# Turning quantised weights with DMA transposes from SBUF to SBUF in a recurrent network with a feed-forward block

## The reference

```python
xW = einsum('ntd,dh->nth', x, Wx) + b               # x: (2, 2048, 512)
h_t = tanh(xW_t + h_{t-1} @ Wh)                     # 2048 steps, h_0 = cond_1024
def quant_linear(x, w, b):                          # w: one scale for each row
    s_in = max(max(x), EPS) / 255;  xq = clip(round(x / s_in), 0, 255) * s_in
    s_w = max(max|w| over a row, EPS) / 127;  wq = clip(round(w / s_w), -128, 127) * s_w
    bq = round(b / (s_in * s_w)) * s_in * s_w
    return xq @ wq.T + bq
hidden = relu(quant_linear(h, w1, b1))              # w1: (2048, 512)
y = x + quant_linear(hidden, w2, b2)                # w2: (512, 2048)
```

## Time and profile before

| | before |
|---|---|
| median of 3 runs | 517.89 us (517.83 to 518.94) |
| the profiled execution | 517.75 us |
| its span | 515.9 us |
| mean granted TensorE clock | 0.996 of full |
| TensorE busy | 496.1 us, 96% of the span |
| VectorE, ScalarE, GpSimd busy | 310.6, 256.5, 55.8 us |
| share of TensorE in the chain that ended last | 93% |

### The profile page before, as it was taken

The page is one execution under the profiler, slowest core; times in us unless marked ns, Lnnn a source line. Parts: engine busy times, 40 slices in busy tenths (PEclk is TensorE's granted clock), DMA queues, the critical chain, the costliest instruction groups (busy, mean ns, idle before and its releaser), DMA issues.

```text
span 515.9 us, 9080 instructions
## 1 busy us (share of the span) xinstructions
PE 496.1 (96%) x2954; PEld 300.8 (58%) x2954; DVE 310.6 (60%) x587; ACT 256.5 (50%) x455; POOL 55.8 (11%) x41
## 2 busy tenths in 40 slices
PE   8999999999999999999857999999998999999997
PEld 3444555555599999999845444444444444444442
DVE  0988880000033344545677988888687687778776
ACT  0434444444233332323478555555554776676661
POOL 2000000000000000000000000000000543534455
PEclk9999999999999999999999999999998999999999
DMA  8988510000000000000000577300002088888883
GB/s 293 323 314 297 176 70 1 0 1 1 0 0 0 0 0 0 0 0 0 1 2 3 213 295 307 164 0 1 0 0 81 2 285 269 304 291 323 287 315 123
DMA packets 21142, 61.19 MB, mean 119 GB/s; under 512 B 2032, under 2 KB 2176, under 8 KB 17536
## 3 DMA queue, kind: packets, MB, share of 16 engines
q1 hardware_dynamic: 20448, 59.84, 31.9%
q10 hardware_dynamic: 576, 1.05, 0.6%
q0 software_dynamic: 96, 0.01, 0.0%
HBM read 39.93 MB, written 20.97 MB: 118 GB/s over the span
## 4 chain that ended last, share of the span: by engine, by line
PE 93%; DVE 3%; ACT 2%; issue 1%; DVEq 0%
PE bank L468 22%; PE bank L637 22%; PE bank L677 21%; PE bank L493 11%; PE bank L499 11%; PE bank L483 3%; PE bank L515 2%; PE bank L448 1%; DVE arena L1037 1%; PE bank L464 1%; ACT arena L824 1%; ACT w1t L737 0%; DVE arena L1238 0%; DVE arena L1262 0%; DVE acc_max L1198 0%
## 5 line engine op out<-in xcount | busy, mean ns | idle before, releaser
L468 PE MATMUL bank<-arena 128*128 128x512 f32 x256 | 116.2, 602 | 0.2 <-DMA arena<-wx 0.2
L637 PE MATMUL bank<-arena,w1t 128*128 128x512 bf16 (+1 forms) x512 | 110.9, 379 | 1.2 <-DVE arena L1167 1.2
L677 PE MATMUL bank<-arena,w2t 128*128 128x512 bf16 x512 | 111.4, 379 | 0.5 <-DVE arena L1262 0.5
L433 POOL TENSOR_SCALAR arena<-arena,bq 128x512 f32<-128x512 f32 x32 | 53.1, 1672 | 446.8 <-DVEq L1283 393.5
L637 PEld LDWEIGHTS bank<-arena,w1t 128*128 128x128 bf16 x512 | 49.9, 98 | 61.9 <-issue 1.4
L677 PEld LDWEIGHTS bank<-arena,w2t 128*128 128x128 bf16 x512 | 49.1, 98 | 62.6 <-DVE arena L1262 4.8
L1198 DVE TENSOR_REDUCE acc_max<-arena 128x2 f32<-128x1024 f32 x60 | 71.6, 1217 | 15.8 <-ACT arena L875 15.2
L468 PEld LDWEIGHTS bank<-arena 128*128 128x128 f32 x256 | 47.3, 192 | 51.4 <-issue 50.3
L875 ACT COPY arena<-bank 128x1024 f32<-128x1024 f32 x56 | 56.7, 1012 | 40.2 <-PE bank L637 40.2
L899 ACT ACTIVATE arena<-arena,bias,scale 128x512 uint16 (+1 forms) x93 | 69.9, 807 | 9.0 <-DVE arena L1250 8.3
L994 DVE TENSOR_TENSOR arena<-bank,arena 128x128 f32 x48 | 14.0, 292 | 91.5 <-PE bank L499 91.2
(11 more groups left out here) (96 smaller groups left out, 314.7 us busy)
## 6 DMA issues: line engine op xcount, KB each, us to landing
spill<-arena SPq DMA_DIRECT2D x12, 1024.0 KB, 3.9
arena<-spill SPq DMA_DIRECT2D x12, 1024.0 KB, 8.9
arena<-w SPq DMA_DIRECT2D x8, 1024.0 KB, 5.3
arena<-x_t SPq DMA_DIRECT2D x32, 256.0 KB, 3.8
y_t<-arena SPq DMA_DIRECT2D x32, 256.0 KB, 2.1
arena<-x_t SPq DMA_DIRECT2D x7, 1024.0 KB, 8.6
arena<-x_t ACTq DMA_DIRECT2D x4, 256.0 KB, 5.8
arena<-wx SPq DMA_DIRECT2D x4, 256.0 KB, 5.2
```

The source lines that it names most:

```text
L433: nc.gpsimd.tensor_scalar(xb[:, d], xb[:, d], bq2[:, d:d + 1], None, ALU.add).then_inc(xb_ready, 1)
L468: return nc.tensor.matmul(bank[:, j, :], wx_sb[:, k, j * P:(j + 1) * P], x_in[:, X_ORDER[i], k, :], start=(k == 0), stop=(k == KT - 1))
L637: mm = nc.tensor.matmul(bank[:, f % 8, :], w1t[:, k, f * P:(f + 1) * P], q[:, slot, k, :], start=(k == 0), stop=(k == KT - 1))
L677: return nc.tensor.matmul(bank[:, 4 + d, :], w2t[:, f, d * P:(d + 1) * P], hq[:, f % HQ_RING, :], start=(f == 0), stop=(f == FT - 1))
```

## The change

- The integers of w1 are written row by row to `w1_ints`, which is the space of `w2t`; those of w2 to `w2_ints`, in the area of the first two x groups that TensorE uses. So VectorE first waits until these 8 units of x products are done.
- SP issues 16 DMA transposes for w1, each 128x512 bf16 from `w1_ints` to `w1t`, four behind each of the x and w2 loads of groups 4 to 7. When all 16 have landed, it issues 4 for w2, each 128x2048 bf16, from `w2_ints` to `w2t`.
- TensorE waits for all of `w2t` before the recurrence, since the states go over `w2_ints`.
- `turn_weights`, `store_turned`, the bf16 identity and their semaphores are gone. In the first joint TensorE does 7, 2 and 5 idle products, in the second 6, 2 and 9, the first 6 ahead of the transpose of `s_hid` and after the last kept bank.

```diff
+IDLE_STATES = (7, 2, 5)
+IDLE_HIDDEN = (6, 2, 9)
+IDLE_BANK = 7
...
+        w1_ints = w2t
+        x_done = x_in[:, X_ORDER[0]:X_ORDER[0] + 2]
+        assert X_ORDER[1] == X_ORDER[0] + 1
+        w2_ints = x_done.bitcast(BF16).rearrange("p g k t -> p (g k t)").rearrange(
+            "p (i f) -> p i f", i=KT)
...
                 load_x(i, i % 2)
                 load_w(i, i % 2, (w_in[:, i % 2, :], w2_v[i - 4]))
 
+                sp.wait_ge(w_int_ready, i - 3)
+                for n in range(4 * (i - 4), 4 * (i - 3)):
+                    nc.sync.dma_start_transpose(w1t[:, :, n * P:(n + 1) * P],
+                                                w1_ints[:, n, :]).then_inc(w1_turned, 16)
+
+            sp.wait_ge(w1_turned, 16 * FT)
+            for i in range(KT):
+                sp.wait_ge(w_int_ready, 4 + i + 1)
+                nc.sync.dma_start_transpose(w2t[:, :, i * P:(i + 1) * P],
+                                            w2_ints[:, i, :]).then_inc(w2_turned, 16)
+
...
             nc.gpsimd.memset(ones[:, :], 1.0).then_inc(ones_set, 1)
-            pool.wait_ge(small_in, 32)
-            nc.gpsimd.tensor_copy(id16[:, :], id32[:, :]).then_inc(id16_set, 1)
...
-                if unit in TURN_BEHIND:
-                    if TURN_BEHIND[unit] == 0:
-                        pe.wait_ge(id16_set, 1)
-                        pe.wait_ge(ones_set, 1)
-                    pe.wait_ge(w_int_ready, TURN_BEHIND[unit] + 1)
-                    for a in range(4):
-                        n = 4 * TURN_BEHIND[unit] + a
-                        turn_weights(n, 4 + a, after=(n - 4 if n >= 4 else None))
...
+            pe.wait_ge(w2_turned, 16 * KT)
             pe.wait_ge(xw_free, KT + GROUPS * KT)
             main_pass(0)
...
-            turn_middle(0, 11)
-            spread_stat(0, lambda: turn_middle(11, 13))
-            turn_middle(13, MIDDLE - EARLY)
+            def keep_going(n):
+                idle_products(n, IDLE_BANK, w1t[:, 0, 0:P], w1t[:, 0, 0:GTOK])
+
+
+            pe.wait_ge(fixed_ready, 2 * FIXED)
+            keep_going(IDLE_STATES[0])
+            spread_stat(0, lambda: keep_going(IDLE_STATES[1]))
+            keep_going(IDLE_STATES[2])
             pe.wait_ge(flag_ready, 1)
...
             all_kept = ACC_RING + GROUPS * PAIRS - len(HELD) // 2
-            pe.wait_ge(acc_kept, all_kept - 1)
-            turn_late(0, 1)
+            pe.wait_ge(acc_kept, all_kept)
+            keep_going(IDLE_HIDDEN[0])
             pe.wait_ge(hid_ready, 1)
             nc.tensor.transpose(bank[0:1, 4, 0:P], s_hid[:, :], id32[:, :]).then_inc(hid_turned, 1)
-            pe.wait_ge(acc_kept, all_kept)
-            turn_late(1, ring)
+            keep_going(IDLE_HIDDEN[1])
             pe.wait_ge(hid_row, 1)
             nc.tensor.matmul(bank[:, 4, P:P + 1], ones[:, :], stat_row[:, 0:1], start=True,
                              stop=True).then_inc(hid_spread, 1)
-            turn_late(ring, TURNED - MIDDLE)
-
-            pe.wait_ge(w_stored, MIDDLE + 2)
-            idle_products(IDLE_BARRIER, LATE_BANKS[1], w1t[:, 0, 0:P], w1t[:, 0, 0:GTOK])
-            pe.wait_ge(w_stored, TURNED)
+            keep_going(IDLE_HIDDEN[2])
             pe.wait_ge(scales1_ready, 1)
...
-            for i in range(MIDDLE - EARLY):
-                store_turned(EARLY + i, MIDDLE_BANKS[i % len(MIDDLE_BANKS)])
             act.wait_ge(flag_ready, 1)
...
-                linked(nc.vector.tensor_scalar(turned, ints, ROUND, None, ALU.subtract), w_link,
+                linked(nc.vector.tensor_scalar(ints, flat, ROUND, None, ALU.subtract), w_link,
                        g * W_LINKS + 6)
...
+            dve.wait_ge(xw_acc, 2 * KT)
             with dve.Fori(2, 4) as half:
                 i = half * 2
                 for par in range(2):
-                    integers(i + par, par, w2_scale, w2_inv, w2_absmax, i + par - 4, 1, 2048)
+                    tile = i + par - 4
+                    integers(i + par, par, w2_scale, w2_inv, w2_absmax, tile, 1,
+                             w2_ints[:, bass.ds(tile, 1), :].rearrange("p a f -> p (a f)"))
```

More of the change, by code:

```diff
@@ L451, in _ @@
             idle_products(IDLE_START, 7, idle_in[:, 0:P], idle_in)
[L453 to L465, removed]
             def x_product(i, j, k):
@@ L584, in _ @@
             pe.wait_ge(h0_in, 16)
+            pe.wait_ge(small_in, 32)
+            pe.wait_ge(ones_set, 1)
+            pe.wait_ge(w2_turned, 16 * KT)
             pe.wait_ge(xw_free, KT + GROUPS * KT)
@@ L588, in _ @@
                 fix_step(t)
[L590 to L599, removed]
-            turn_middle(0, 11)
-            spread_stat(0, lambda: turn_middle(11, 13))
-            turn_middle(13, MIDDLE - EARLY)
+            def keep_going(n):
[4 more added lines that the diff above has]
+            keep_going(IDLE_STATES[2])
             pe.wait_ge(flag_ready, 1)
             def repair(r):
-                pe.wait_ge(w_stored, MIDDLE)
                 pe.wait_ge(seams_moved, r)
@@ L629, in first_products @@
                         tiles.sort(key=lambda t: t[1])
-                    if first and pair == 1:
-                        pe.wait_ge(w_stored, MIDDLE)
                     for f, k in tiles:
@@ L731, in evacuate_tile @@
                                      ACT.Identity, bias=b_sb[:, j:j + 1]).then_inc(xw_free, 1)
[L733 to L740, removed]
             def guess_pair(s, a):
@@ L789, in _ @@
                         evacuate_tile(0, to)
-                if unit in TURN_BEHIND:
-                    for a in range(4):
-                        store_turned(4 * TURN_BEHIND[unit] + a, 4 + a)
             def exact_tanh(n, src, dst):
@@ L885, in _ @@
                                    bank[:, f % 8:f % 8 + 2, :]).then_inc(acc_kept, 1)
-                if pair == PAIRS - 2:
-                    store_turned(MIDDLE, LATE_BANKS[0])
-            for i in range(1, TURNED - MIDDLE):
-                store_turned(MIDDLE + i, LATE_BANKS[i % len(LATE_BANKS)])
             act.wait_ge(scales1_ready, 1)
@@ L936, in _, with integers @@
             W_LINKS = 6
-            def integers(g, par, scales, inverses, absmax, first, n, width):
+            def integers(g, par, scales, inverses, absmax, first, n, ints):
                 dve.wait_ge(w_landed[par], g * 8 + (16 - 8 * par))
@@ L956, in integers @@
                                                ALU.max, ALU.min), w_link, g * W_LINKS + 5)
-                if n == 4:
-                    turned = w1t[:, :, bass.ds(first * P, n * P)].rearrange(
-                        "p k (a c) -> p a k c", a=n)
-                    ints = flat.rearrange("p (a k c) -> p a k c", a=n, c=P)
-                else:
-                    turned = w2t[:, :, bass.ds(first * P, P)]
-                    ints = flat.rearrange("p (a c) -> p a c", c=P)
-                linked(nc.vector.tensor_scalar(turned, ints, ROUND, None, ALU.subtract), w_link,
+                linked(nc.vector.tensor_scalar(ints, flat, ROUND, None, ALU.subtract), w_link,
                        g * W_LINKS + 6)
@@ L972, in _ @@
                 for par in range(2):
-                    integers(i + par, par, w1_scale, w1_inv, w1_absmax, (i + par) * 4, 4, 512)
+                    first = (i + par) * 4
+                    integers(i + par, par, w1_scale, w1_inv, w1_absmax, first, 4,
+                             w1_ints[:, bass.ds(first, 4), :].rearrange("p a d -> p (a d)"))
             dve.wait_ge(wh_in, 16)
```

13 lines of the change are left out of this document (3 added, 10 removed).

## The result

| | before | changed |
|---|---|---|
| median of 5 runs | 517.83 us (517.71 to 518.94) | 515.16 us (513.18 to 516.14) |
| the profiled execution | 517.75 us, span 515.9 | 513.50 us, span 511.7 |

The ratio of the times is 0.9946 with a 95% interval of 0.9919 to 0.9972, so the changed kernel is faster by about 0.5%. 515.9 was forecast.

A forecast was written before the change was run, and what follows sets the result against it. TensorE's long pieces of products and the two joints were taken to bound the kernel. Terms -2.67 + 0 - 0.57 + 1.35 = -1.89 took 517.75 us to 515.9, range 514.0 to 519.3.

The forecast's parts named there:

- TensorE transposes behind the x products, -2.67: Between x products: removing three pieces of 16 weight transposes, 0.89 us each, starts the recurrence 2.67 us earlier.
- The DMA transposes, cost 0: Before the recurrence: the new w1 and w2 transposes take about 27 us, hidden within 99.8 us of x products.
- upper bounds of 132 and 172 us: DMA transposes: 132 us if short packets cost the old mean packet, 172 us if 20 DMAs land one after another.
- Late x loads, VectorE's wait, cost 0: During x products: x loads issued behind transposes and VectorE's wait for units 0 to 7 delay nothing; cost 0.
- The first joint, -0.57: Between recurrence and first products: the statistics' transpose no longer waits behind weight transposes, 0.57 us earlier; bounds nothing to -0.7.
- The second joint, +1.35 or -0.17: Between first and second products: 6 idle products delay s_hid; +1.35 us if the clock falls (taken), -0.17 at full clock.
- The sum: Whole kernel: -2.67 + 0 - 0.57 + 1.35 = -1.89 us, from 517.75 to 515.9 us.
- Serial pieces: Rival before the recurrence: DMA transposes run one after another and TensorE waits for w2t; 548 or 588 us, chance 0.16.
- The clock holds: Rival in the second joint: the clock stays full, -0.17 there, 514.3 us in all; chance 0.25.
- The clock costs more: Rival in the joints: clock returns late in the second (517.6 us) or also falls in the first (both 519.3); chance 0.12.

The follow-up runs named there:

- The first trace: The changed kernel unedited, its profiled execution from the five runs of the result, with the clock at 1.00 through the second joint: 513.50 us.
- two more rounds: The four w2 DMA transposes issued three times over, on the changed kernel with second-joint idle products ahead of the last kept bank: 511.90 us, ratio 0.9886.
- ten rounds: The four w2 DMA transposes issued ten times over, each round after the one before landed, on the changed kernel: 574.24 us.
- the two versions with idle products ahead: Changed kernel with 8 or 7 second-joint idle products ahead of the last kept bank, none between it and the s_hid transpose: 512.16 and 512.65 us.

## Why the prediction was right, step by step

**TensorE transposes behind the x products, -2.67.** Right. The first trace shows 3.81, and the missing 1.1 us is no part of the change: before's x products took 44.40 us and that trace's 43.35, which differ as much between traces of the same code (43.15 to 44.49). Against the trace with 44.49 the recurrence starts at 135.65, 138.33 - 135.65 = 2.68. Putting small products back gave the same 2.67 in pieces.

**The DMA transposes, cost 0.** Right, and the value taken for them (27 us) was near. The SP queue had 17024 more packets and the 16 engines 0.379 x 511.7 - 0.319 x 515.9 = 29.4 us more of packet time, so a short packet costs 29.4 x 16 / 17024 = 0.028 us where the mean one of before cost 0.129. The upper bounds of 132 and 172 us came from rows that were too far: the short packet cost less than a quarter of the long one, and DMAs in one queue didn't wait for each other's landing (they were issued every 1.5 to 2.1 us and landed after 5 to 6). That 27 us came so near is luck in part, as it was a choice between bounds of 13.6 and 132. By the 1309 ns for a 128x128 block (the Trainium skill, VectorE: DVE Perf Modes, "The three transpose paths") an estimate for a round of w2, 64 blocks that never overlap, is 84 us; the trace has 11.7 with the landing. The 261 GB/s that the Trainium skill gives for one kernel (DMA: Bandwidth & Descriptors, "Latency and other measured facts") is nearer; in the windows from 74 to 84 us, where the w2 transposes ran, the trace has 186 to 215. That the wait costs nothing while it is covered and its full length beyond was right too: two more rounds cost nothing, and with ten rounds the recurrence was 58.3 us late and the end 60.7.

**Late x loads, VectorE's wait, cost 0.** Right: an x load 7 us later, no gap in the products.

**The first joint, -0.57.** Right. From the start of the recurrence to the last reduction before was 393.61 - 138.33 = 255.28, after 254.64 and 254.62 in the two traces, 0.65 less; the forecast was 0.57. Timeline of the changed kernel, as in the earlier trace rows:

```profile
274.18 0.15 DVE L1037 TENSOR_REDUCE stat<-seam_max 128x1 f32<-128x4 f32 x1
...
274.38 0.38 PE L562 MATMUL bank<-id,stat 128*1 128x128 f32 x2 [0.35 <-DVE stat L1037]
...
276.36 0.16 DVE L1050 TENSOR_SCALAR s_in<-bank 128x1 f32<-128x1 f32 x1 [0.97 <-PE bank L567]
```

The transpose starts 0.05 us after the statistics and not 0.68.

**The second joint, +1.35 or -0.17.** Both happen. Where the clock falls it is 8.51 - 6.96 = +1.55 (1.35 forecast); where it holds 6.97 - 6.96 = +0.01 (-0.17 forecast). The choice of the falling clock was right for 12 of 17 executions, and the share of the other, 5 of 17, is near the 0.25 that the rival had. What the prediction did not see is that the kernel before has the same choice: its trace is one in which the clock fell, and of its 65 executions in these studies 11 are below 516, the same 11 of 60 that have a mean clock of 0.999 or more. So the reason that the prediction gave for the fall, the longer idle piece of 2.4 us, doesn't carry it: with pieces of 0.69 and 1.32 us and transposes between them before fell in 49 of 60, the changed kernel in 12 of 17. The chance of 0.25 that it gave to a clock that holds was about right; that came without the right reason, so it is luck in part. The joint that before would have at full clock is taken as 5.87 us, measured with five idle products added; no trace of before itself has it. So the change made this joint longer in both cases, by 1.55 with the clock fallen in both and by 1.1 with it held in both, and gave back here between a third and a half of the 3.3 us that it won.

**The sum.** For the trace in which the clock falls: -2.68 - 0.66 + 1.55, and 0.2 less behind the joint, is -2.0, which is 513.9 against 515.9 of span. The forecast was -1.89. By the medians more was gained: 2.6 us where the clock fell in both (517.92 and 515.31), 2.0 where it held in both (515.15 and 513.18), 2.7 over all, so 515.16 came out where 515.9 was forecast. Part of the difference is that 24 of the 49 fallen executions of before have a mean clock of 0.993 and a median of 518.28, and of the twelve of the changed kernel one has 0.993; against the other 25 of before (517.61) it is 2.3. No trace of before shows such an execution, nor why its two groups lie 2.8 us apart where the joint differs by 1.1. Both stay open.

**Rivals.** Serial pieces: refuted (the packet row and the ten rounds). The clock holds: true for a third of the executions, 513.50 for the first trace where 514.3 was forecast, the 0.8 less being mostly the quicker start (1.1 us). The clock costs more: no traced execution of the changed kernel has it, and none of the 17 reaches 517. Without the first idle products of the second joint the clock did stay at half through the last nine, and without those of the first joint it fell there.

## What to carry to other kernels

Ask of a TensorE operation that leaves the chain whether TensorE was busy on both sides: only then is its time the gain, and here it was exactly that. A transfer that replaces it is free up to a deadline that can be read off the old trace, so bound its price from both sides and compare it with the deadline before looking for its value. Idle products that keep the clock belong into the wait, ahead of the operation that ends it, into a bank that is already free; behind it they stand on the path and may come after the clock has fallen. If another engine's work hangs on what stands behind them, as the weight copy did in the kernel before, they delay that. And one trace of each kernel is too little where the clock falls in some executions only: compare groups of the same clock.

## What the runs showed of the hardware

- With an idle piece of 2.4 us in the second joint TensorE's clock fell to half (1.2 GHz) in 12 executions and held in 5 of the same kernel. The fall came 2.1 us into a piece of 2.50 in one trace, 1.2 us into one of 2.61 behind the repair steps in another, and in a third 0.5 us behind one of 2.42. The Trainium skill (TensorE: Matmul & The Clock Gate, "Why this matters for your kernels") advises against idle gaps between bursts of products; the traces agree, and show falls with shorter gaps than the one it names.
- The length of one idle piece doesn't settle it. With 0.69 us at most in that joint, and idle products in it, the clock held in all 11 executions of the two versions with idle products ahead, and in 3 of the 4 with three rounds of w2 transposes (where it fell in the fourth isn't known). With the same longest piece, but with transposes standing in the joint, it held in 5 of 12. In the first joint a piece of 1.58 us passed at 1.00, and so did 6 us of before in which TensorE did nearly only transposes; in the repair steps it fell once with pieces of 1.50 and 0.69.
- The first 100 x-product instructions took 43.15 to 44.49 us, the same code in seven traces. A pair of traces can differ by 1.3 us from this alone. The durations fit a clock that rises sooner or later; the granted clock of the windows doesn't show it.
- A DMA transpose of 128x512 bf16 held SP's queue for 1.2 to 2.9 us (1.5 in the median), and one of 128x2048, four times the data, for 1.8 to 3.6 (2.1); a plain load of 1 MB beside them held it for 0.34 to 0.72. The x loads behind them went out up to 7 us later and had the time here; a queue whose loads are needed at once would feel it.
